# A shifted-window attention block with a convolution behind it: where the Gelu table is loaded, and in which order the transposed strip is stored

## The reference

```
xn   = layer_norm(x)                                  # over the 96 channels
wins = 7x7 windows of roll(xn, (-3, -3))              # 16 x 256 windows of 49 tokens
q, k, v = split(wins @ qkv_w + qkv_b)                 # 3 heads of 32
attn = softmax(scale * q @ k.T + rel_bias + mask)     # 49 x 49 per window and head
x1   = x + roll_back(windows_back(attn @ v) @ proj_w + proj_b)
x2   = x1 + gelu_tanh(layer_norm(x1) @ fc1_w + fc1_b) @ fc2_w + fc2_b    # 96 -> 384 -> 96
out  = batch_norm(pointwise(depthwise3x3(relu(x2)) + dw_bias) + pw_bias)
```

## Time and profile before

| what | us |
|---|---|
| time, median of 3 runs (6512.4 to 6515.14) | 6512.81 |
| the profiled execution's own time | 6517.97 |
| its span, first to last instruction | 6516.1 |
| TensorE matmul, busy | 5792.5 (89%) |
| VectorE, busy | 5509.5 (85%) |
| ScalarE, busy | 5348.5 (82%) |
| GpSimd, busy | 3807.6 (58%) |

### The profile page before, as it was taken

How to read it: one execution, slowest core, us unless ns; L and a number is a source line. 1 busy time by engine, 2 the same in 40 slices (tenths; PEclk the granted TensorE clock), 3 DMA queues, 4 the chain that set the end, 5 groups by cost and what they waited for, 6 DMA issues and landing times.

```text
span 6516.1 us, 202567 instructions
## 1 busy us (share of the span) xinstructions
PE 5792.5 (89%) x81170; PEld 4049.6 (62%) x81170; DVE 5509.5 (85%) x13747; ACT 5348.5 (82%) x11040; POOL 3807.6 (58%) x4105
## 2 busy tenths in 40 slices
PE   6889898888989888988898989888889898988887
PEld 4666666666666666666666666666666666666665
DVE  4888888888888888888888888888888888888887
ACT  5888888888888888888888888888888888888886
POOL 3655555556565655555656565555565656565563
PEclk9999999999999999999999999999999999999998
DMA  0010101010101010101010101010101010110100
GB/s 21 24 28 24 28 24 28 24 28 24 28 24 28 24 28 24 28 24 28 24 28 24 28 24 28 24 28 25 28 24 28 25 27 26 26 26 26 26 26 20
DMA packets 250521, 167.92 MB, mean 26 GB/s; under 512 B 220423, under 2 KB 220920, under 8 KB 249592
## 3 DMA queue, kind: packets, MB, share of 16 engines
q1 hardware_dynamic: 249592, 154.97, 9.2%
HBM read 77.81 MB, written 77.07 MB: 24 GB/s over the span
## 4 chain that ended last, share of the span: by engine, by line
PE 31%; POOL 24%; ACT 18%; DVE 17%; issue 10%; SPq 1%; DVEq 0%; DMA 0%; ACTq 0%; POOLq 0%
POOL prob L857 12%; PE bank L425 8%; ACT hT L564 7%; POOL rstd L863 6%; PE bank L457 5%; DVE stats L767 5%; ACT L508 5%; PE bank L374 5%; POOL x1n L873 4%; PE bank L357 4%; DVE x L803 4%; PE bank L442 3%; PE bank L469 3%; PE bank L410 3%; DVE ssum L727 2%
## 5 line engine op out<-in xcount | busy, mean ns | idle before, releaser
L751 DVE SCALAR_TENSOR_TENSOR acc<-ymap,taps,acc 96x784 f32<-96x784 f32 (+2 forms) x2176 | 2557.0, 1180 | 45.7
L863 POOL TENSOR_TENSOR rstd<-var_eps,minus_half 112x7 f32<-112x7 f32 x512 | 937.1, 1830 | 2378.1 <-DVE var_eps L782 2378.1
L374 PE MATMUL bank<-x1T,w 96*128 96x448 f32 (+1 forms) x3072 | 1143.6, 509 | 97.6 <-ACT hT L564 95.7
L393 PE MATMUL bank<-hT,w 128*96 128x448 f32 (+1 forms) x3072 | 1095.5, 492 | 0.0
L857 POOL TENSOR_TENSOR prob<-prob,srec 128x392 f32<-128x392 f32 x768 | 811.9, 1087 | 212.6 <-DVE srec L729 211.5
L374 PEld LDWEIGHTS bank<-x1T,w 96*128 96x128 f32 x3072 | 541.7, 189 | 565.7 <-issue 463.8
L873 POOL TENSOR_SCALAR xn<-x_in,minus_mean,rstd 112x96 f32<-112x96 f32 x768 | 844.8, 1111 | 0.0
L564 ACT ACTIVATE hT<-bank,bfc 128x448 f32<-128x448 f32 (+1 forms) x1536 | 824.6, 576 | 14.6 <-PE bank L374 2.2
L848 POOL TENSOR_TENSOR prob<-prob,smax 128x392 f32<-128x392 f32 x768 | 804.1, 1077 | 20.8 <-DVE smax L720 20.8
L727 DVE TENSOR_REDUCE ssum<-prob 128x8 f32<-128x392 f32 x768 | 403.9, 526 | 391.0 <-ACT prob L508 391.0
L410 PE MATMUL bank<-ident,prob 113*113 113x113 f32 x3072 | 476.6, 278 | 243.2 <-POOL prob L857 236.5
(11 more groups left out here) (88 smaller groups left out, 11065.6 us busy)
## 6 DMA issues: line engine op xcount, KB each, us to landing
out<-o_tile SPq DMA_DIRECT2D x256, 210.0 KB, 2.5
x_in<-in_x SPq DMA_DIRECT2D x256, 168.0 KB, 2.9
x_in<-in_x SPq DMA_DIRECT2D x256, 126.0 KB, 3.3
out<-o_tile SPq DMA_DIRECT2D x256, 84.0 KB, 2.5
hT<-in_L_conv_rel_bias SPq DMA_DIRECT2D x49, 0.6 KB
x1T<-in_L_conv_fc_w SPq DMA_DIRECT2D x1, 144.0 KB, 2.5
w<-in_L_conv_fc_w SPq DMA_DIRECT2D x1, 144.0 KB, 2.3
hT<-in_L_conv_qkv_w SPq DMA_DIRECT2D x1, 108.0 KB, 2.1
```

Of the source, the lines that this page charges most:

```text
L374: pe.matmul(bank[(5, 6, 0)[m]][:, 0:n * PT_], w1[:, m * 128:(m + 1) * 128], x1T[:, first * PT_:(first + n) * PT_], start=True, stop=True). ...
L393: mm = pe.matmul(bank[b][0:C, 0:n * PT_], w2[:, m, :], hT[:, m, first * PT_:(first + n) * PT_], start=False, stop=(m == MC - 1))
L751: last = dve.scalar_tensor_tensor(out=dst, in0=src, scalar=taps[:, i:i + 1], in1=dst, op0=ALU.mult, op1=ALU.add)
L863: pool.tensor_tensor(b["rstd"][:], b["var_eps"][:], minus_half[0:PT_], ALU.pow)\
```

## The change

Three places change together, and what they compute stays the same.

The dummy Gelu activation moves from the head of `gelus` to the head of ScalarE's step, ahead of the query copies. Queries, keys, x1n, x1T and the first o_tile copy now run while Gelu's table is loaded; they ran under Exp's.

The copies into xT become straight: xT now holds the strip as it stands in PSUM, 49 positions x 16 windows with the window innermost.

TensorE's three sets of matmuls read xT through a view that puts the windows back in order: `windows[:, w, n]` is element n * 16 + w. Queries and keys read 8 windows x 49 positions as moving operand with a step of 16 elements (64 bytes); values read 49 elements with the same step as stationary operand. What they write, and in which order, is as before.

```diff
--- before.py
+++ after.py
@@ -315,16 +315,18 @@
                                            qT[hp, at], kT[hp, at], start=True, stop=True)
                 mm.then_inc(s_psum, 1)
 
+            windows = xT[:].rearrange("p (n w) -> p w n", w=NWIN)
+
             def queries_keys(t):
                 if not has(t + 1):
                     return
                 wait(pe, xt_ready, nth(t + 1, 2, 1))
                 for u in range(2):
-                    pe.matmul(bank[3 + u][0:C, 0:HALF], wqkv[:, 0:C], xT[:, u * HALF:(u + 1) * HALF],
+                    pe.matmul(bank[3 + u][0:C, 0:HALF], wqkv[:, 0:C], windows[:, u * PAIRS:(u + 1) * PAIRS],
                               start=True, stop=True).then_inc(q_psum, 1)
                 for u in range(2):
                     wait(pe, x1_ready, nth(t - 1, 2, u))
-                    pe.matmul(bank[5 + u][0:C, 0:HALF], wqkv[:, C:2 * C], xT[:, u * HALF:(u + 1) * HALF],
+                    pe.matmul(bank[5 + u][0:C, 0:HALF], wqkv[:, C:2 * C], windows[:, u * PAIRS:(u + 1) * PAIRS],
                               start=True, stop=True).then_inc(k_psum, 1)
 
             def values(t, i):
@@ -340,7 +342,7 @@
                             w = 4 * q + 2 * odd + side
                             at = (2 * (q % 2) + side) * C
                             mm = pe.matmul(bank[(7, 3)[i]][64 * odd:64 * odd + NT, at:at + C],
-                                           xT[:, w * NT:(w + 1) * NT], wqkv[:, 2 * C:], start=True, stop=True)
+                                           windows[:, w], wqkv[:, 2 * C:], start=True, stop=True)
                 mm.then_inc(v_psum, 1)
 
             def turn_x1(t):
@@ -555,7 +557,6 @@
                 if not has(t - 1):
                     return
 
-                act.activation(table_load[:, 1:2], table_load[:, 0:1], ACT.Gelu_apprx_tanh)
                 wait(act, y_psum, nth(t - 2, 2, 1))
                 for i in range(2 * MC):
                     half, m = i // MC, i % MC
@@ -595,9 +596,7 @@
                 first, n, b = ((0, 4, 3), (4, 3, 4))[i]
                 wait(act, v_psum, nth(t + 1, 2, 1))
                 wait(act, xt_psum, nth(t + 2, 2, i))
-                src = bank[b][0:C, 0:n * PT_].rearrange("p (n w) -> p n w", w=NWIN)
-                dst = xT[:].rearrange("p (w n) -> p n w", w=NWIN)[:, first * WS:(first + n) * WS, :]
-                act.copy(dst, src).then_inc(xt_ready, 1)
+                act.copy(xT[:, first * PT_:(first + n) * PT_], bank[b][0:C, 0:n * PT_]).then_inc(xt_ready, 1)
 
             def into_map(t, half):
                 if not has(t - 1):
@@ -621,6 +620,8 @@
                 last.then_inc(ymap_ready, 1)
 
             def step(t, phase):
+                if has(t - 1):
+                    act.activation(table_load[:, 1:2], table_load[:, 0:1], ACT.Gelu_apprx_tanh)
                 queries(t)
                 keys(t, 0)
                 keys(t, 1)
```

## The result

The changed kernel takes 7936.8 us (median of 4 runs, 7929.0 to 7958.5) against 6512.6: 1.219 times as long, 95% interval 1.217 to 1.222. The forecast was 6975 us, with a range to 7060. The sign and the mechanism it named are there; 962 us are not in it.

A forecast was written before the change was run, and what follows sets the result against it. No engine was the bound but a loop of hand-overs over four, 25.04 us a step. 256 x (+2.64 - 0.84) = +461 us on 6517.97 gave 6979, less the profiled run's 5.2 us excess 6974, rounded 6975; range 6320 to 7060.

The forecast's parts named there:

- The table load: Gelu load moved ahead of ScalarE's query copies: gains 0.71 us a step, between 0 and 0.85.
- The straight copy: ScalarE's copies into xT: saves ScalarE 0.80 us a step, worth nothing by itself on the chain.
- The stationary reads: Values' 32 weight loads on TensorE: up to 0.46 us extra, hidden in idle time; bounds 0 and 1.33 us.
- rival 2: Moving and stationary reads both double, weight loads don't overlap: +2.67 us a step, 7197 us; chance 0.14.
- The moving reads: Queries' and keys' eight passes on TensorE double, 2.64 us more a step; bounds 0 and 3.2 us.
- there is no cover: Behind the queries and keys: nothing hides their extra 2.64 us, so keys and then hidden come that much later.
- hidden starts at 3017.20 + 2.64 = 3019.84: Start of hidden on TensorE: 2.64 us later, putting the Exp load at 3024.42 against 3022.63, some 1.80 us later.
- The sum: Whole kernel: 256 x (+2.64 - 0.84) = +461 us on the profiled 6517.97 us, 6979 us, forecast as 6975.

The follow-up runs named there:

- e3_moving: The changed kernel with the values matmuls reading xT straight as weights, queries and keys still with a step of 16; 7946 us.
- e4_weights: The changed kernel with queries and keys reading xT straight, only the values' weight loads keeping the step of 16; 6370 us.
- e12_split: The changed kernel with keys behind the values on TensorE and x1n ahead of the key copies on ScalarE; 6954.9 us, ratio 1.067.
- e9_idle: All matmul reads straight, but TensorE waits for VectorE's second biased score tile before it starts the queries; 8408 us.
- e10_apart: The changed kernel with the keys behind the values on TensorE, x1n in its old place on ScalarE; 8371 us.
- e7_queries: The straight kernel, but the queries alone read xT with the step of 16, keys straight; 6656 us.
- the straight kernel: The changed kernel with all three matmul sets reading xT straight, tokens in another order; table move and straight copy stay; 6372 us.

## Why the prediction was wrong

- **The table load: right, a little large.** 0.59 us a step against 0.71; the six Gelus end 0.22 us later after hidden's start than I worked out. Identity and Copy run under Gelu's table with no further load: 256 Gelu and 255 Exp loads as before.
- **The straight copy: right.** 944 to 531 ns, and nothing in time (6372 against 6367 us).
- **The stationary reads: right.** Nothing on the chain. The sign that I gave for rival 2, a row of loads far above 1.7 us, did appear (2.49 us) and misled: e3_moving and e4_weights show that it came from the clock.
- **The moving reads: right in size, partly by luck.** 0.65 to 0.66 us a pass. At full clock, with keys and x1n in their new places, they cost 6955 - 6367 = 588 us or 2.3 us a step where I had 2.64; in the old order four of the eight cost 6656 - 6372 = 284 us, 1.07 a step where half of my 2.64 is 1.32. So "there is no cover" was a little wrong. The reason given was luck: I took an SBUF read on TensorE from an SBUF write on ScalarE, whose stepped PSUM read turned out all but free and whose stepped SBUF read no run shows, and I let a pass double "whenever an element lies away from its neighbour", which the step of 8 bytes refutes (0.34 us).
- **The failed step is "hidden starts at 3017.20 + 2.64 = 3019.84", and behind it "The sum".** It let every pass behind the keys keep its duration: hidden to start 2.64 us later after the queries and the Exp load 1.80. They start 4.54 us later (10.96 against 6.42) and 5.67 (17.52 against 11.85). I read 1.00 in the clock column as a fact of the kernel; it held for that order and those reads only. Eight stepped passes, 5.4 us in one piece, take it to 1.2 GHz for some 10 us, over values, turn_x1, pointwise and most of hidden, all on the chain. That the clock falls because the array does too little in such a stretch is the reading that fits all the kernels here; what exactly counts as little, they don't show.

By the two kernels' timelines, the stretch from the queries' start to the Exp load grew from 11.85 to 17.52 us: queries and keys 2.81 to 5.42, values with the wait behind them 1.99 to 2.74, turn_x1 0.84 to 1.33, pointwise 0.78 to 1.47, hidden and Gelus 5.43 to 6.56 (with the table loaded ahead it would have been 4.82). In whole times: -145 us (table, 6367 against 6513), +588 us (doubled passes), +982 us (the clock, 7937 against 6955; the two differ in the order of keys, values and x1n too, so this is the clock's price only as far as that order costs nothing itself). The three are differences along a row of kernels, so they add up to the whole, 1424 us, by construction; that proves nothing about the shares.

The range's upper end, 7060, lay 85 us above the forecast, and even rival 2, left out at 7197, was a term of the same kind: more passes or loads at the old speed. No rival let the clock move, though the price was in reach: any TensorE work on the chain, doubled.

## What to carry to other kernels

A float32 operand that TensorE streams should have two elements within 16 bytes, as the step of 8 bytes had; where a reordering must be paid, ScalarE reading PSUM with the step does it for next to nothing here, and the stepped weight loads were hidden. When a change makes TensorE's passes wait or leaves it a stop, price the work behind at half clock as a case of its own; the busy share won't show it, so read the granted clock by stretches. If slow passes can't be avoided, try putting dense ones between them: here that brought back 982 us.

## What the runs showed of the hardware

- A float32 pass over 392 columns takes 0.33 us straight, 0.34 with a step of 8 bytes, 0.69 with 16, 0.66 with 64, at full clock; stepped passes take 0.65 at half clock too (e12_split at 1341.93), where straight ones take 0.67 (e9_idle, 2.69 for four). The two halvings don't multiply.
- In this step the clock fell in a stop of 2.69 us with straight reads (e9_idle), in a stop of 1.87 us right behind four stepped passes (e10_apart), and at the end of eight stepped passes in one piece, 5.4 us. It stayed full over four of them, 2.67 us (e7_queries), and over eight with the values between, 7.05 us (e12_split). Stops of 0.81 and 0.89 us stand in every step of the straight kernel and leave it full. These are places in this kernel, not limits. The Trainium skill's "TensorE: Matmul & The Clock Gate", section "Part 1: The HAM clock gate (the "warmup" mystery)", has it that a monitor sets the array's clock by how busy the array has been lately, and names two states, 1.2 and 2.4 GHz; the stretches agree with the two, 1.00 and 0.50, with mixed values only where the edge falls inside one. The profile's busy share isn't that measure: TensorE is shown busy for all of the 5.4 us ahead of the fall.
- ScalarE pays about 1.0 ns an element for a stepped SBUF write and 0.02 ns (540 against 531 ns for 448) for a stepped PSUM read with straight writes.
